# Fixed-point attention: rounded query and key projections for groups three to eight, and one odd unit in four turned by ScalarE

## The reference, cut to what matters

```python
SCALE = 4096.0; EPS = 1.0 / SCALE; CLIP_VAL = 8
def make_fxp(x):
    c = CLIP_VAL - EPS
    x = jnp.clip(x, -c, c)
    return jnp.trunc(x * SCALE) / SCALE
qkv = jnp.einsum('bnd,ed->bne', x, w_qkv)
q, k, v = ...                      # split in heads, each make_fxp'd
dots = make_fxp(jnp.einsum('bhnd,bhmd->bhnm', q, k) * scale)
attn = make_fxp(make_fxp(jax.nn.softmax(dots, axis=-1)))
out = make_fxp(jnp.einsum('bhnm,bhmd->bhnd', attn, v))
out = make_fxp(make_fxp(jnp.einsum('bne,de->bnd', out, w_proj) + b_proj))
```

## Time and profile before

| what | value |
|---|---|
| median of 3 runs | 1651.45 us (1649.7 to 1653.36) |
| profiled execution, its time | 1653.62 us |
| profiled execution, its span | 1652.3 us |
| PE busy | 1550.6 us (94%) |
| DVE busy | 1121.1 us (68%) |
| ACT busy | 917.0 us (55%) |
| POOL busy | 486.9 us (29%) |
| the stage `l2_attn` | from about 535 to 837 us of the span |

### The profile page before, as it was taken

One profiled execution on the slowest core, in us unless ns is written; L12 is line 12 of the kernel. 1 busy time (PEld: TensorE's weight loads), 2 busy tenths in 40 slices (PEclk: granted clock), 3 DMA queues, 4 the chain that ended last, 5 costly groups with the idle time before them and its releaser, 6 DMA issues.

```text
span 1652.3 us, 23165 instructions
## 1 busy us (share of the span) xinstructions
PE 1550.6 (94%) x7819; PEld 855.8 (52%) x7819; DVE 1121.1 (68%) x2250; ACT 917.0 (55%) x1758; POOL 486.9 (29%) x567
## 2 busy tenths in 40 slices
PE   8999998989998999999979999999988989999998
PEld 3477753458873444444335555555344444545446
DVE  7766764876447899999568888887377526665515
ACT  5432443533346777778457777787325645555613
POOL 0220500130001555555115655665020103323300
PEclk9999999999999999999989999999998999999999
DMA  6000210120010000000254311110165020000000
GB/s 246 0 1 21 75 52 0 38 77 1 26 46 0 20 10 11 11 11 30 102 182 131 106 30 30 44 44 20 46 163 166 25 83 24 13 22 12 1 1 26
DMA packets 40044, 80.45 MB, mean 49 GB/s; under 512 B 4539, under 2 KB 25531, under 8 KB 38235
## 3 DMA queue, kind: packets, MB, share of 16 engines
q1 hardware_dynamic: 39926, 78.97, 14.8%
HBM read 62.08 MB, written 16.78 MB: 48 GB/s over the span
## 4 chain that ended last, share of the span: by engine, by line
PE 71%; DVE 12%; issue 7%; ACT 6%; DMA 1%; SPq 1%; POOL 1%; PEldq 1%; PEld 0%; DVEq 0%; POOLq 0%; ACTq 0%
PE ps L2614 6%; PE ps L2196 3%; PE ps L3533 3%; PE ps L2172 3%; PE ps L2603 3%; PE ps L2218 3%; PE ps L3498 3%; PE ps L3508 3%; PE ps L3553 2%; PE ps L240 2%; PE ps L2625 2%; PE ps L2182 2%; PE ps L3526 2%; PE ps L3566 2%; PE ps L2629 2%
## 5 line engine op out<-in xcount | busy, mean ns | idle before, releaser
L2869 POOL TENSOR_TENSOR work<-work,arena_b 128x512 f32<-128x512 f32 x128 | 168.0, 1314 | 118.2 <-ACT work L2733 118.2
L2823 DVE CUSTOM_DVE_ANT_0 work<-ps,arena_a 128x1024 f32<-128x1024 f32 x128 | 154.8, 1210 | 0.6 <-PE ps L2614 0.3
L2715 ACT ACTIVATE work<-work,small 128x1024 f32<-128x1024 f32 x128 | 146.8, 1147 | 3.9 <-DVE small L2823 3.9
L2614 PE MATMUL ps<-identity,work 128*128 128x128 f32 x1024 | 140.8, 280 | 6.6 <-DVE work L2835 2.1
L2614 PEld LDWEIGHTS ps<-identity,work 128*128 128x128 f32 x1024 | 116.9, 144 | 55.1 <-issue 29.3
L3715 POOL TENSOR_SCALAR ctx_keys<-ctx_keys,small 128x128 f32<-128x128 f32 (+3 forms) x128 | 67.2, 539 | 171.2 <-DVE small L3640 171.2
L2835 DVE TENSOR_TENSOR work<-ps,arena_b 128x512 f32<-128x512 f32 x128 | 88.0, 687 | 34.2 <-PE ps L2614 31.4
L2733 ACT ACTIVATE work<-ps 128x512 f32<-128x512 f32 x128 | 76.3, 596 | 60.3 <-PE ps L2614 56.8
L2388 POOL TENSOR_SCALAR work<-work 128x1024 f32<-128x1024 int32 x64 | 66.7, 1042 | 100.6 <-DVE work L2343 100.2
L2603 PE MATMUL ps<-work 96*128 96x512 bf16 x256 | 80.2, 396 | 13.1 <-DVE small L2823 7.4
L3592 ACT ACTIVATE ctx_keys<-ctx_keys,small 128x128 f32<-128x128 f32 (+3 forms) x128 | 70.8, 555 | 28.5 <-DVE small L3632 28.0
(11 more groups left out here) (471 smaller groups left out, 3614.8 us busy)
## 6 DMA issues: line engine op xcount, KB each, us to landing
work<-parts_k_L_xattn SPq DMA_DIRECT2D x14, 384.0 KB, 4.0
ctx_feat<-in_ctxT SPq DMA_DIRECT2D x2, 2048.0 KB, 19.2
ctx_keys<-in_ctx_keys SPq DMA_DIRECT2D x2, 2048.0 KB, 16.5
arena_a<-in_mask SPq DMA_DIRECT2D x2, 2048.0 KB, 7.7
arena_b<-in_groupT SPq DMA_DIRECT2D x2, 2048.0 KB, 9.6
head_weights<-in_w_L_xattn SPq DMA_DIRECT2D x8, 449.0 KB, 3.3
arena_a<-in_w_l_attn SPq DMA_DIRECT2D x1, 3072.0 KB, 15.1
head_weights<-in_w_L_attn SPq DMA_DIRECT2D x8, 384.0 KB, 3.1
```

Of the source, the lines that this page charges most:

```text
L2614: mm = pe.transpose(t_psum[z][:, kt * P:(kt + 1) * P], prob[i % NP][:, o:o + P], k.iden[:, :])
L2715: act.activation(p, p, ACT.Exp, scale=-1.0, bias=minmax[:, i % 8:i % 8 + 1], accum_out=sums[:, i % 8:i % 8 + 1]).then_inc(*exped.up())
L2823: dve.tensor_tensor_reduce(prob[i % NP], s_psum[i % NS], NEG[:, b, qt, :], -1.0, BIG * 3e8, OP.add, OP.min, minmax[:, i % 8:i % 8 + 1]).th ...
L2869: pool.tensor_tensor(p, p, GT[:, b, 4:8, qt * P:(qt + 1) * P], OP.mult).then_inc(*weighed_pool.up())
```

## The change

It does four things.

1. For groups 2 to 7 (the third to the eighth) a query or key chunk is made of six matmuls on float32r operands in place of two on float32. Each operand is split in a rounded part ("high") and the remainder ("low"); the chunk is high by high plus low weights by high input plus high weights by low input, for each half of the features.
2. The parts have to be made. The input's high parts are four copies on ACT at steps 2 to 5, its low parts four subtractions on DVE at steps 3 to 6. The weights' high part is a copy on POOL in step 6 of group g - 2, right behind the scaling, which moves there from step 0 of group g - 1; the low part is a subtraction on DVE in step 7 of group g - 2, between L2343 and L2352.
3. The turn of a unit whose number leaves three when divided by eight is done by ACT in place of DVE.
4. The input's high parts lie over `k.extra`, so SP loads the next stage's weights there again after the last chunk, and `l2_xattn` waits for that load.

```diff
+    x_high = view(k.rounded("heads_x_high", "extra", 0, DC * NT), 0, DC, NT)
+    x_low = view(k.rounded("heads_x_low", "spare", 0, DC * NT), 0, DC, NT)
+    w_high = [k.rounded(f"heads_w_high_{s}", "norm_parts", S * s, S) for s in range(2)]
+    w_low = [k.rounded(f"heads_w_low_{s}", "spare", DC * NT + S * s, S) for s in range(2)]
+    PARTS = 2
...
+    on_act = lambda i: i % 2 == 0 or i % 8 == 3
+    turned = lambda i: (turned_act if on_act(i) else turned_dve)(sum(on_act(y) == on_act(i) for y in range(i + 1)))
...
         sp.wait_ge(*part(len(CHUNKS)))
+        k.ahead["values"].reload(sp)
         thin_loads(k, sp, "L2_xattn")
...
                 if i >= 2:
-                    pe.wait_ge(*(turned_odd if i % 2 else turned_even)(i // 2))
+                    pe.wait_ge(*turned(i - 2))
...
+                elif g >= PARTS:
+                    s, j = g % 2, what == "k"
+                    pe.wait_ge(*x_rest(4))
+                    pe.wait_ge(*w_rest(g - PARTS + 1))
+                    for c in range(DC):
+                        pe.matmul(c_bank(x), W_high[s][j][:, c, :], x_high[:, c, half(n)], start=c == 0, stop=False)
+                        pe.matmul(c_bank(x), W_low[s][j][:, c, :], x_high[:, c, half(n)], start=False, stop=False)
+                        mm = pe.matmul(c_bank(x), W_high[s][j][:, c, :], x_low[:, c, half(n)], start=False, stop=c == 1)
                 else:
...
+            if 2 <= step < 6:
+                n, c = divmod(step - 2, DC)
+                act.wait_ge(*ln.out(n + 1))
+                act.activation(x_high[:, c, half(n)], k.Hn[:, c, half(n)], ACT.Copy).then_inc(*x_top.up())
             i = step - 6
-            if 0 <= i < N and i % 2 == 0:
+            if 0 <= i < N and on_act(i):
...
+            if 3 <= step < 7:
+                n, c = divmod(step - 3, DC)
+                dve.wait_ge(*x_top(step - 2))
+                dve.tensor_tensor(x_low[:, c, half(n)], k.Hn[:, c, half(n)], x_high[:, c, half(n)].bitcast(F32),
+                                  OP.subtract).then_inc(*x_rest.up())
+            if step >= 0 and step % per == 7 and step // per + 2 < G:
+                g = step // per + 2
+                dve.wait_ge(*w_top(g - PARTS + 1))
+                dve.tensor_tensor(w_low[g % 2][:, :], weights[g % 2][:, 0:S], w_high[g % 2][:, :].bitcast(F32),
+                                  OP.subtract).then_inc(*w_rest.up())
             i = step - 6
-            if 0 <= i < N and i % 2:
+            if 0 <= i < N and not on_act(i):
...
-            if step < -5 or (step >= per and step % per == 0 and step // per + 1 < G):
-                g = step + 7 if step < 0 else step // per + 1
+            if step < -5 or (step >= 0 and step % per == 6 and step // per + 2 < G):
+                g = step + 7 if step < 0 else step // per + 2
                 pool.wait_ge(*w_in[g % 2](g // 2 + 1))
                 pool.tensor_scalar(weights[g % 2], weights[g % 2], FX, 0.0, OP.mult, OP.add).then_inc(*w_scaled.up())
+                if g >= PARTS:
+                    pool.wait_ge(*w_scaled(g + 1))
+                    pool.tensor_scalar(w_high[g % 2][:, :], weights[g % 2][:, 0:S], 1.0, 0.0, OP.mult, OP.add).then_inc(*w_top.up())
...
+    def reload(self, sp):
+        sp.dma_start(self.k.extra[:, 0:2048], self.k.a["w_L2_xattn"]).then_inc(*self.loaded.up())
```

More of the change, by code:

```diff
@@ L2093, in l2_attn @@
     W = [[view(x, 256 * j, 2, P) for j in range(3)] for x in weights]
+    x_high = view(k.rounded("heads_x_high", "extra", 0, DC * NT), 0, DC, NT)
+    x_low = view(k.rounded("heads_x_low", "spare", 0, DC * NT), 0, DC, NT)
+    w_high = [k.rounded(f"heads_w_high_{s}", "norm_parts", S * s, S) for s in range(2)]
+    w_low = [k.rounded(f"heads_w_low_{s}", "spare", DC * NT + S * s, S) for s in range(2)]
+    W_high, W_low = ([[view(x, 256 * j, 2, P) for j in range(2)] for x in ws] for ws in (w_high, w_low))
+    PARTS = 2
     sums = [k.small[:, 2 * j:2 * j + 2] for j in range(4)]
@@ L2122, in l2_attn @@
     part, scored, turn, pv, final = k.signals("pe", 5)
-    part_sign, signed, exped, turned_even, out_sign, fin, fin_sign = k.signals("act", 7)
-    ready, part_int, truncated, inverse, whole, turned_odd, out_int, fin_step, resid = k.signals("dve", 9)
-    w_scaled, q_clipped, part_fixed, clipped, summed, out_put = k.signals("pool", 6)
+    part_sign, signed, exped, turned_act, out_sign, fin, fin_sign, x_top = k.signals("act", 8)
+    ready, part_int, truncated, inverse, whole, turned_dve, out_int, fin_step, resid, x_rest, w_rest = k.signals("dve", 11)
+    w_scaled, q_clipped, part_fixed, clipped, summed, out_put, w_top = k.signals("pool", 7)
     masks = Masks(k) if nxt else None
@@ L2189, in tensor @@
                     pe.wait_ge(*part_fixed(made(g, "v")))
-                    pe.wait_ge(*turned_even(2 * j + 2))
-                    pe.wait_ge(*turned_odd(2 * j + 2))
+                    pe.wait_ge(*turned(nk * j + 2))
+                    pe.wait_ge(*turned(nk * j + 3))
+                    pe.wait_ge(*turned(nk * j + 1))
                     if j:
@@ L2281, in scalar @@
                 act.activation(PT[j % 2][:, :, :, qt * P:(qt + 1) * P],
-                               t_bank[0].bitcast(I16).rearrange("p (h k t) -> p h k t", h=nh, t=P), ACT.Identity,
-                               scale=1.0 / FX, bias=back).then_inc(*turned_even.up())
+                               t_bank[i % 2].bitcast(I16).rearrange("p (h k t) -> p h k t", h=nh, t=P), ACT.Identity,
+                               scale=1.0 / FX, bias=back).then_inc(*turned_act.up())
             i = step - 11
@@ L2352, in vector @@
                 dve.tensor_scalar(PT[j % 2][:, :, :, qt * P:(qt + 1) * P],
-                                  t_bank[1].bitcast(I16).rearrange("p (h k t) -> p h k t", h=nh, t=P),
-                                  -float(OFFSET), 1.0 / FX, OP.add, OP.mult).then_inc(*turned_odd.up())
+                                  t_bank[i % 2].bitcast(I16).rearrange("p (h k t) -> p h k t", h=nh, t=P),
+                                  -float(OFFSET), 1.0 / FX, OP.add, OP.mult).then_inc(*turned_dve.up())
             i = step - 11
@@ L2580, in tensor @@
         pe.wait_ge(*loaded(3))
+        pe.wait_ge(*raw.loaded(2))
         if not hoisted:
```

## The result

Five runs of the changed kernel gave a median of 1657.66 us (1655.84 to 1659.72), five of the kernel before 1650.98 (1649.7 to 1653.36): a ratio of 1.0032 [1.0016, 1.0047]. Two later timings of the same two kernels gave 1.0000 [0.999, 1.001] (12 and 35 runs) and 1.0022 [1.0011, 1.0033] (12 and 19 runs). Weighted by the runs of the changed kernel that is 1.0015, 2.4 us slower. So the change costs a little or nothing; the mean lies within the 0.2% that can't be told from none, the first and the third timing beyond it, with intervals that leave out 1. The first median lies 1.2 us above the range that I gave, and 6 us above the time.

What follows compares the result with a forecast made beforehand. PE waits on ACT's chains in steps 2, 3, 6 and 7, while steps 4 and 5 are PE's own. −5.4 (chunks) + 3.05 (w_low) + 2.5 (start) = +0.15 us, forecast 1651.5 us, range 1645.5 to 1656.5.

Steps and rivals of the forecast that it cites:

- chunks: Query and key chunks, six matmuls each: only steps 4 and 5 gain, 0.9 us a group, 5.4 us in all.
- w_low: Weights' remainder, subtracted on DVE in step 7: delays step 0's transposes by 0.61 us, 3.05 us over five steady groups.
- start: First group, up to the start of step 12: making the parts costs 2.5 us, bounds 0.6 to 3.7.
- pairs of steps: Steps 2 and 3, and 6 and 7, of a steady group: still 7.1 us a pair after the change.
- What bounds it: Steady group of 32.66 us: ACT sets steps 2, 3, 6 and 7; steps 4 and 5 are PE's own.
- ACT's chains: ACT's gapless work through steps 2 and 3, and 6 and 7: 7.14 us from P(2), not shortened by the change.
- P(4) and P(0): Starts of PE's steps 4 and 0 in a group of eight; PE waits there, about 0.2 us at P(4).
- Six take 1.40: Six float32r matmuls of a chunk at 0.233 us each take 1.40 us instead of 1.89, saving 0.49 a chunk.
- The turned unit: Unit 3's turn, moved from DVE's to ACT's step 1 in steady groups: 1.12 us hidden on ACT, no gain in itself.
- POOL first: Rival: DVE's subtractions wait for POOL's clip of 1.04 us; +7.3 us, 1659, chance 0.12.
- x_low: Input's remainders, four DVE subtractions in steps 3 to 6 of the first group: 4 × 0.61 = 2.44 us.
- POOL's copy and the reload: Weights' rounding copy in step 6, about 0.61 us, costing nothing or at most 0.1; reload of "extra", 10.9 us, hidden.

Runs made afterwards that it cites:

- after_again: The changed kernel as it is, timed once more against the kernel before: ratio 1.0000, stage 247.21 us.
- filler: The changed kernel with eight unread matmuls in PE's step 7 of the first group, where PE waits for DVE: ratio to the kernel before 1.0001.
- short_sign: The changed kernel with ACT's sign over 8 of 512 columns for every output but the first (outputs not right): 1651.0 us, one run.
- late_exp: `both`, with ACT's two exponentials behind the sign of the scores in every fourth step: 1647.72 us, ratio to the kernel before 0.9971.
- before_late_exp: The kernel before with ACT's two exponentials behind the sign of the scores in every fourth step, nothing else: 1654.35 us, one run.
- wlow_behind: The changed kernel with the weights' low part subtracted behind the turn in step 7, not in front: ratio to the kernel before 1.0003.
- turn_only: The kernel before with only unit 3 of each group turned by ACT: ratio to the kernel before 1.0004.
- both: The changed kernel with the changes of wlow_behind and x_early together: 1648.37 us, ratio to the kernel before 0.9974.
- x_early: The changed kernel with the input's high and low parts made four steps earlier: ratio to the kernel before 0.9998.

## Why the prediction was right and wrong

**The sum by its terms**, for the stage without a fall of the clock: chunks −3.9 (six times 0.65), w_low +3.0 (five times 0.61), start +1.96, pairs of steps −0.1: +1.0. Measured are 247.21 − 246.11 = +1.10 (after_again) and +1.11 (filler). The forecast had −5.4 + 3.05 + 2.5 = +0.15.

- *What bounds it*: right. PE waits for ACT's chains at P(4) and P(0); the pairs stayed at 7.13 and 7.12. short_sign and late_exp show the chain to be ACT's, before_late_exp that DVE is next: PE then waited 0.37 for it.
- *The chunks*: right in kind (steps 4 and 5 alone pay), too large in size. "Six take 1.40" took the distance inside a stream of twelve. For the change of operand kind I took off 0.02, a term that no row shows. The runs showed 0.19 in its place: the first load isn't ahead of its matmul and the first distance is 0.34, the last, to the float32 matmul behind, 0.32, and the six take 1.59. That is 0.33 a step for 0.47, 0.65 a group for 0.9, 1.5 us in all. This is the step of the sum that failed.
- *w_low*: right. 0.68 long, 0.61 later at the transposes, five times; given back by wlow_behind to the hundredth.
- *The start*: right in kind, somewhat too dear. Units 0 to 8 cost 1.96 for the 2.7 of my first terms. Each subtraction pushed DVE by 0.61 as said, but its multiplications got 0.23 shorter when POOL was the one held up, so that steps 4, 5 and 7 are longer by 0.38 to 0.40 and not by 0.6; step 3 is longer by 0.14, and step 6 by 0.66. From unit 8 to unit 12 both kernels take 15.25: the turn's 0.7 (forecast 0.6) pays for the first w_low.
- *The turned unit*: right, hidden on ACT, nothing in groups.
- *POOL first* (the slower rival): it didn't happen. w_low never exceeded 0.69, and three of the four x_low took 0.68; the other, the third, met POOL's copy already under way and took 0.97. DVE starts 0.16 before POOL's clip (556.00 and 556.16), and POOL's 0.38 had slack. The Trainium skill, "GPSIMD Engine Reference", Key points, names the contention; the trace agrees (1.04 became 1.42) and adds who pays here. By it I had the start at 2.5 or more; it cost 1.96.
- *POOL's copy and the reload*: L2418 took 0.62 as estimated, but I had its price on PE as nothing, at most 0.1, and in the first group that was wrong. There it stood in the way of the third x_low, and step 6 grew by 0.66, which is 0.28 more than steps 5 and 7. In steady groups I found no wait that it left on PE, and none from the reload.
- *Not in the prediction at all*: the clock. I counted what the subtractions add to PE's wait (1.93 before, then 2.31 and 0.61) as time alone. In seven of eight traces with a longer or an additional wait ahead of step 8's score matmul or transposes the granted clock fell there; in none of the six others (before, turn_only, both, late_exp, before_late_exp, filler). What sets it off stays open: after_again had the same waits and no fall, filler keeps the 0.61 behind a wait of 0.59 and had none, x_early fell with 1.93 and 0.40, and late_exp didn't with 1.93 and, a step later, 1.30. It adds 1.0 to 1.5 to step 8, of which the next steps, with slack of their own, give half back: 44.03 − 43.31 = +0.7 by unit 12.

That makes +1.1 without and +1.8 with that fall. The rest of the 6.1 of the first pair is 2.6 ahead of the stage, which is the clock's of that run (unit 0 starts at 539.4 to 544.9 in the fourteen traces, sorted by the granted clock and not by the kernel), and 1.8 behind it. There the clock fell again at 830 to 850, in six of the seven traces that had the first fall and in no other; the part behind unit 63 averaged 866.3 in those six and 863.9 in the eight others. Why the one should follow the other 260 us later is open. With both falls the change costs about 4 us, with neither about 1, and 1.0015 lies between. That the total came out within 0.2% is in part luck: the sum for the stage was short by 1 us, and the clock, which moves the total by more than that from run to run, wasn't in it.

## What to carry to other kernels

Before a cheaper matmul is counted, look at each step for what ends last, and price it between the neighbours that it will have, not inside a stream of its own kind. Put preparatory work on an in-order queue behind the instruction that another engine waits for, and at a time when that engine is idle anyway: the same work in other places turned +1 us into −3.8 in the stage. A change that lengthens a wait of TensorE may cost more than the wait, if the clock falls behind it; and where the clock falls in other stages from run to run, the stage's own time tells more than the total.

## What the hardware showed that I had not expected

- Where a wait had grown from 1.93 to 2.31, mostly with 0.61 behind it, TensorE's clock came down in most traces, and sixteen matmuls took 3.08 for 2.05. The Trainium skill, "TensorE: Matmul & The Clock Gate", HAM oscillation — how this bites in real kernels, describes waits that bring the lower clock on the work behind them. Its waits are for DMA, these are for VectorE; the traces agree in seven of eight, and filler, which fills the wait, is in line with it in its one trace and doesn't prove it.
- GpSimd's clip of 128x1024 takes 1.42 instead of 1.04 when VectorE has begun a subtraction of two SBUF operands just before it, and that subtraction keeps its 0.68.
- A float32r matmul over 512 columns costs 0.23 in a stream, but 0.34 as the first behind a float32 one, and 0.31 behind bfloat16 transposes.
- In parts of the program that no kernel changed, the clock fell in some executions and not in others; ahead of the stage alone this moved unit 0 between 539.4 and 544.9 us.
